# Local attention: the scores of all eight heads in one run with the four masks behind them, minima and exponentials of a step ahead of the copies

## The chip, the core and the metric

The program runs on one core of one Trainium2 chip. The core's engines each execute their own list of instructions strictly in the order written: TensorE (PE in the rows; its weight loads are PEld), VectorE (DVE), ScalarE (ACT), GpSimd (POOL) and SyncE (SP), which issues transfers. The engines are tied to each other by semaphores alone. The metric is the device time of one execution in microseconds.

## What is computed

The reference is a decoder of twelve sublayers on x of 2 x 1024 tokens and 256 features. The change touches the attention inside one of them, L2_ffn, which has two layers of local attention followed by a gated network. Cut to that attention (HEADS = 8, DIM_HEAD = 64, WINDOW = 128, two layers, two sequences):

```python
q = l2norm(q) * qs; k = l2norm(k) * ksc
q, k = rotary_xpos(q, k)
bq = q.reshape(b, h, w, WINDOW, d) * QK_SCALE
...                      # bk, bv: the block before and the block itself
sim = jnp.einsum('bhwid,bhwjd->bhwij', bq, bk)
mask = (i < j) | (i > j + WINDOW) | (j == -1)
sim = jnp.where(mask, -jnp.finfo(sim.dtype).max, sim)
attn = jax.nn.softmax(sim, axis=-1)
out = jnp.einsum('bhwij,bhwjd->bhwid', attn, bv)
```

A block of 128 queries sees the 128 keys of its own block and the 128 before it; the first block sees its own alone.

## The kernel before

The twelve sublayers run one after the other, each made of phases. Within a phase every engine has its own list, and a phase ends with all of them. `local_attention` is such a phase, called four times: for two layers and in each for two sequences, always behind `local_qkv`, which makes QT, KT (queries and keys, features on the partitions, scaled so that the scores have their sign turned) and V.

It goes over NTB = 8 blocks t of 128 queries. The eight heads are four pairs g, and the pairs are two halves G (pairs 0 and 1, pairs 2 and 3). In a step the work on one block is:

- `score(t, G)` on TensorE (line 3542): for two pairs and two heads of each, q times k of 256 keys (128 in step 0) into the four banks 0 to 3, two for each half. Two heads of a pair lie on different rows of the array. Behind them two masks (line 3546, in step 0 line 3549), a bf16 identity times the window mask over the whole bank. It waits for the exponentials of the step before (`exp_done`), since they read the same banks.
- `minima(t, G)` on VectorE (line 3598): the row minimum from a bank with its mask, two a half.
- `exps(t, G)` on ScalarE (line 3655): four a half, from the bank into `probs`, with the row sums beside them. The read of the accumulated sum is an instruction of its own in the rows.
- `recip(t, G)` on VectorE (line 3605), one for a half, and the product with it on GpSimd (line 3641), one for each pair.
- `turn(t, g)` on TensorE (line 3560): four transposes of one pair's probabilities into bank 4 (pairs 0 and 2) or bank 5 (pairs 1 and 3). It waits for the product (`normed`), and until the pair that used the bank before has been copied out (`pt_out_even`, `pt_out_odd`).
- `take_turned(n)`, n = 4 t + g: that copy, of pairs 0 and 2 on VectorE (line 3612), of pairs 1 and 3 on ScalarE (line 3663).
- `values(t)` on TensorE (line 3572): probabilities times V into bank 6 or 7, one step later. `take_out(t)` on VectorE (line 3616) copies the bank to OT.

The order of each list is written out by hand. TensorE's at step t: score(t+1, 0), turn(t, 0), turn(t, 1), score(t+1, 1), values(t-1), turn(t, 2), turn(t, 3). VectorE's: minima(t, 0), the copy of pair 0 of step t-1, minima(t, 1), recip(t, 0), the copy of pair 2 of step t-1, recip(t, 1), take_out(t-2). ScalarE's: exps(t+1, 0), the copy of pair 1 of step t, exps(t+1, 1), the copy of pair 3 of step t.

Of the kernel before, what the change touches and what calls it, by code (L numbers as in the profile page):

```python
# [23 lines left out]
P = 128  # L24
# [3329 lines left out]
LH, LHD = 8, 64  # L3354
# [160 lines left out]
def local_attention(nc, K, b, QT, KT, V, window_mask, OT):  # L3515


    NTB = S // P
    HALVES = LM // 2
    with ExitStack() as es, phase(nc, K.sems, "scored min_done exp_done recip_done normed turned pt_out_even pt_out_odd pv_done out") as (block, s):  # L3520
# [4 lines left out]
        pairs_of = lambda G: (2 * G, 2 * G + 1)  # L3525
# [3 lines left out]
        def turned_probs(n):  # L3529
            t, g = divmod(n, LM)  # L3530
            return (v.rearrange("p (h k) -> p h k", h=2)[:, :, keys(t)] for v in (K.bank[4 + n % 2][:], PT[:, t % 2, g, :]))

        @block.tensor
        def _(pe):
            def score(t, G):
                ks = keys(t)
                if t:
                    pe.wait_ge(s["exp_done"], LH * (t - 1) + 4 * (G + 1))
                for g in pairs_of(G):
                    for hh in range(2):  # L3540
                        own = slice(hh * LHD, (hh + 1) * LHD)
                        pe.matmul(K.bank[2 * G + hh][:, (g % 2) * 2 * P + ks.start:(g % 2 + 1) * 2 * P], QT[own, g, t * P:(t + 1) * P],
                                  KT[own, g, t * P - P + ks.start:(t + 1) * P], start=(g % 2 == 0), stop=False, skip_group_check=True)
                for hh in range(2):
                    if t:
                        ins = pe.matmul(K.bank[2 * G + hh][:], K.identb[:], window_mask[:], start=False, stop=True, skip_group_check=True)  # L3546
                    else:
                        for half in range(2):
                            ins = pe.matmul(K.bank[2 * G + hh][:, half * 2 * P + P:(half + 1) * 2 * P], K.identb[:], window_mask[:, ks],
                                            start=False, stop=True, skip_group_check=True)  # L3550
                    ins.then_inc(s["scored"], 1)

            def turn(t, g):
                n = LM * t + g
                pe.wait_ge(s["normed"], n + 1)
                if n >= 2:
                    pe.wait_ge(pt_out[n % 2], n // 2)
                for hh in range(2):
                    for kt in ((0, 1) if t else (1,)):
                        ins = pe.transpose(K.bank[4 + n % 2][:, (2 * hh + kt) * P:(2 * hh + kt + 1) * P], Pr[:, t % 2, 2 * g + hh, kt * P:(kt + 1) * P], K.ident[:])  # L3560
                ins.then_inc(s["turned"], 1)

            def values(t):
                kts = (0, 1) if t else (1,)
                for g in range(LM):
                    pe.wait_ge(pt_out[g % 2], (LM * t + g) // 2 + 1)
                    if g == 0 and t >= 2:
                        pe.wait_ge(s["out"], t - 1)
                    for hh in range(2):
                        for kt in kts:  # L3570
                            h = 2 * g + hh
                            ins = pe.matmul(K.bank[6 + t % 2][hh * LHD:(hh + 1) * LHD, g * P:(g + 1) * P], V[:, t - 1 + kt, h * LHD:(h + 1) * LHD],
                                            PT[:, t % 2, g, (2 * hh + kt) * P:(2 * hh + kt + 1) * P], start=(kt == kts[0]), stop=(kt == 1))
                    ins.then_inc(s["pv_done"], 1)

            for G in range(HALVES):
                score(0, G)
            for t in range(NTB):
                if t + 1 < NTB:
                    score(t + 1, 0)  # L3580
                for g in pairs_of(0):
                    turn(t, g)
                if t + 1 < NTB:
                    score(t + 1, 1)
                if t:
                    values(t - 1)
                for g in pairs_of(1):
                    turn(t, g)
            values(NTB - 1)

        @block.vector
        def _(dve):
            def minima(t, G):
                if G == 0 and t >= 2:
                    dve.wait_ge(s["exp_done"], LH * (t - 1))
                for hh in range(2):
                    dve.wait_ge(s["scored"], 2 * (HALVES * t + G) + hh + 1)
                    dve.tensor_reduce(stat[:, t % 2, 0, 4 * G:4 * G + 4].rearrange("p (g hh) -> p hh g", hh=2)[:, hh, :],  # L3598
                                      K.bank[2 * G + hh][:].rearrange("p (h k) -> p h k", h=2)[:, :, keys(t)], AX, ALU.min).then_inc(s["min_done"], 1)

            def recip(t, G):
                dve.wait_ge(s["exp_done"], LH * t + 4 * (G + 1))
                if G == 0 and t >= 2:
                    dve.wait_ge(s["normed"], LM * (t - 1))
                dve.reciprocal(stat[:, t % 2, 2, 4 * G:4 * G + 4], stat[:, t % 2, 1, 4 * G:4 * G + 4]).then_inc(s["recip_done"], 1)  # L3605

            def take_turned(n):
                dve.wait_ge(s["turned"], n + 1)
                if n >= 2 * LM:
                    dve.wait_ge(s["pv_done"], n - 2 * LM + 1)  # L3610
                src, dst = turned_probs(n)
                dve.tensor_copy(dst, src).then_inc(s["pt_out_even"], 1)

            def take_out(t):
                dve.wait_ge(s["pv_done"], LM * (t + 1))
                dve.tensor_copy(OT[:, :, b * S + t * P:b * S + (t + 1) * P], K.bank[6 + t % 2][:].rearrange("p (g k) -> p g k", g=LM)).then_inc(s["out"], 1)

            for t in range(NTB):
                minima(t, 0)
                if t:  # L3620
                    take_turned(LM * (t - 1))
                minima(t, 1)
                recip(t, 0)
                if t:
                    take_turned(LM * (t - 1) + 2)
                recip(t, 1)
                if t >= 2:
                    take_out(t - 2)
            for n in (LM * (NTB - 1), LM * (NTB - 1) + 2):
                take_turned(n)  # L3630
            take_out(NTB - 2)
            take_out(NTB - 1)
# [10 lines left out]
        @block.scalar  # L3643
        def _(act):
            def exps(t, G):
                ks = keys(t)
                if t >= 2:
                    act.wait_ge(s["turned"], LM * (t - 2) + 2 * (G + 1))
                    act.wait_ge(s["recip_done"], HALVES * (t - 2) + G + 1)
                for hh in range(2):  # L3650
                    act.wait_ge(s["min_done"], 2 * (HALVES * t + G) + hh + 1)
                    for g in pairs_of(G):
                        h = 2 * g + hh
                        c0 = (g % 2) * 2 * P
                        act.activation(Pr[:, t % 2, h, ks], K.bank[2 * G + hh][:, c0 + ks.start:c0 + ks.stop], ACT.Exp, bias=stat[:, t % 2, 0, h:h + 1],  # L3655
                                       scale=-1.0, accum_out=stat[:, t % 2, 1, h:h + 1]).then_inc(s["exp_done"], 1)

            def take_turned(n):
                act.wait_ge(s["turned"], n + 1)
                if n >= 2 * LM:  # L3660
                    act.wait_ge(s["pv_done"], n - 2 * LM + 1)
                src, dst = turned_probs(n)
                act.activation(dst, src, ACT.Copy).then_inc(s["pt_out_odd"], 1)

            for G in range(HALVES):
                exps(0, G)
            for t in range(NTB):
                for G in range(HALVES):
                    if t + 1 < NTB:
                        exps(t + 1, G)  # L3670
                    take_turned(LM * t + 2 * G + 1)


# [224 lines left out]
```

## Time and profile before

| | us |
|---|---|
| median of 3 runs | 3375.57 |
| lowest and highest | 3375.1, 3379.15 |
| the profiled execution, whole time | 3380.29 |
| its span, first to last instruction | 3378.5 |
| mean granted TensorE clock, as a share of full speed | 0.913 |
| TensorE busy | 2841.4 (84%) |
| VectorE busy | 1865.6 (55%) |
| ScalarE busy | 1601.3 (47%) |
| GpSimd busy | 676.7 (20%) |

The shares are means over twelve sublayers with different limits. What a change inside one phase is worth has to be read from the rows of that phase. A busy TensorE means that matmuls are in flight; they overlap, so the distance between the starts of two of them is what one costs, and the duration of one is longer. The clock is a share of 2.4 GHz, and a stretch at 0.5 runs at 1.2 GHz.

### The profile page before, as it was taken

The page shows a single profiled execution, that of the slowest core. Times are in us where ns is not written, and L with a number is a line of the kernel's source. Part 1 is how long each engine was busy: PE and PEld are TensorE (multiplying, and loading weights), DVE is VectorE, ACT ScalarE, POOL GpSimd, SP SyncE. Part 2 cuts the span into 40 slices and gives each one's busy share as a digit, 9 for nine tenths or more (in the row PEclk, how much of TensorE's full clock was granted, in tenths as well). Part 3 has the DMA queues.
Part 4 walks back from the last instruction along what each step waited for, and adds up shares of the span by engine and source line. Part 5 has one row for each costly group of instructions (what it writes and reads, how often), then busy time and mean ns, then how long its engine had stood idle before and what let it go on. Part 6 is the DMA issues. An engine that isn't in the chain of part 4 may idle for free. (4 is left out here: it accounts for less than half of the span.)

```text
span 3378.5 us, 53803 instructions
## 1 busy us (share of the span) xinstructions
PE 2841.4 (84%) x18568; PEld 1727.8 (51%) x18569; DVE 1865.6 (55%) x4547; ACT 1601.3 (47%) x4391; POOL 676.7 (20%) x757
## 2 busy tenths in 40 slices
PE   7788948638999998679979998999988889959992
PEld 4634633414555555346645563355634356639992
DVE  5655763624887885667656642266423648633333
ACT  5335942314777774772235542155421539713331
POOL 3110020112121120012116630066300003201113
PEclk9879979769999999889999999999999989959996
DMA  1010020010000001000010000000000000141112
GB/s 69 2 18 1 2 82 0 7 62 1 2 2 2 2 2 38 25 13 2 17 40 1 1 34 28 6 1 1 1 28 13 6 23 2 37 197 36 36 35 82
DMA packets 35171, 80.64 MB, mean 24 GB/s; under 512 B 8897, under 2 KB 23826, under 8 KB 30834
## 3 DMA queue, kind: packets, MB, share of 16 engines
q1 hardware_dynamic: 30002, 64.68, 5.3%
q0 software_dynamic: 4368, 11.93, 1.2%
q8 instruction: 137, 2.24, 0.3%
q10 hardware_dynamic: 560, 0.93, 0.1%
q14 instruction: 104, 0.85, 0.1%
HBM read 63.18 MB, written 14.02 MB: 23 GB/s over the span
## 5 line engine op out<-in xcount | busy, mean ns | idle before, releaser
L2459 ACT ACTIVATE scores<-scores,min 128x128 f32<-128x128 f32 (+7 forms) x256 | 198.4, 775 | 86.6 <-DVE min L2442 82.8
L2440 DVE TENSOR_SCALAR zero_marks<-psum 128x128 f32<-128x128 f32 (+7 forms) x256 | 192.1, 751 | 67.9 <-PE psum L2372 65.6
L2442 DVE CUSTOM_DVE_ANT_0 scores<-psum,zero_marks 128x128 f32<-128x128 f32 (+7 forms) x256 | 194.0, 758 | 29.9 <-issue 0.9
L2379 PE MATMUL psum<-ident,scores 128*128 128x128 f32 x1152 | 173.1, 277 | 16.8 <-ACT probsT L2476 13.9
L2476 ACT ACTIVATE probsT<-psum 128x128 f32<-128x128 f32 (+7 forms) x256 | 163.0, 637 | 32.9 <-PE psum L2379 32.3
L3783 PE MATMUL psum<-Hn,W 128*128 128x512 f32 x384 | 169.5, 605 | 8.7 <-PEq L415 8.7
L1597 ACT ACTIVATE XT<-psum,b_of_tile 128x128 f32<-128x128 f32 x312 | 89.0, 368 | 178.8 <-PE psum L1517 178.8
L1517 PE MATMUL psum<-x_gatheredT,XT 128*128 128x128 f32 x1248 | 153.3, 283 | 6.1 <-issue 3.2
L1517 PEld LDWEIGHTS psum<-x_gatheredT,XT 128*128 128x128 f32 x1248 | 148.4, 198 | 12.9 <-issue 11.8
L2379 PEld LDWEIGHTS psum<-ident,scores 128*128 128x128 f32 x1152 | 123.4, 141 | 56.3 <-issue 29.9
L2369 PE MATMUL psum<-XT,Q_heads 64*128 64x512 f32 x256 | 143.7, 641 | 0.0
L3641 POOL TENSOR_TENSOR probs<-probs,stat 128x512 f32<-128x512 f32 (+1 forms) x128 | 123.2, 986 | 98.7 <-DVE stat L3605 96.3
L1526 PE MATMUL psum<-W,XT 128*128 x624 | 141.2, 379 | 0.6 <-DVE y L1571 0.6
L3655 ACT ACTIVATE probs<-psum,stat 128x256 f32<-128x256 f32 (+1 forms) x256 | 114.4, 461 | 47.0 <-DVE stat L3598 45.0
L3783 PEld LDWEIGHTS psum<-Hn,W 128*128 128x128 f32 x384 | 74.3, 194 | 103.9 <-issue 103.9
L3509 POOL TENSOR_TENSOR straight<-straight,crossed 128x512 f32<-128x512 f32 x64 | 81.1, 1268 | 225.2 <-DVE crossed L3499 225.2
L1526 PEld LDWEIGHTS psum<-W,XT 128*128 128x128 f32 x624 | 115.5, 190 | 15.1 <-issue 1.0
L3799 DVE SCALAR_TENSOR_TENSOR GT<-psum,b,gelu 128x512 f32<-128x512 f32 x48 | 36.1, 752 | 141.5 <-ACT gelu L3793 141.5
L848 ACT ACTIVATE probs<-probs,stat 128x154 f32<-128x154 f32 x256 | 104.9, 412 | 2.0 <-DVE stat L786 2.0
L3598 DVE TENSOR_REDUCE stat<-psum 128x2 f32<-128x512 f32 (+1 forms) x128 | 78.2, 653 | 49.4 <-PE psum L3546 27.6
L2370 PE MATMUL psum<-XT,Q_heads_turned 64*128 64x128 f32 (+3 forms) x256 | 102.8, 482 | 0.0
L2363 PE MATMUL psum<-XT,Q_heads 128*128 128x128 f32 (+3 forms) x256 | 97.1, 462 | 3.5 <-POOL Q_heads L2341 2.8
(623 smaller groups left out, 6756.4 us busy)
## 6 DMA issues: line engine op xcount, KB each, us to landing
W<-in_L3f_W SPq DMA_DIRECT2D x16, 1024.0 KB, 22.4
L3f_y_rows<-y SPq DMA_DIRECT2D x39, 128.0 KB, 1.7
L0f_rows<-Xtok SPq DMA_DIRECT2D x2, 2048.0 KB, 7.7
W<-in_L0f_W SPq DMA_DIRECT2D x3, 1152.0 KB
early_weights<-in_L2f_Wqkv SPq DMA_DIRECT2D x2, 1536.0 KB
W<-in_L2f_W SPq DMA_DIRECT2D x2, 1536.0 KB
XT<-in_xT SPq DMA_DIRECT2D x1, 2048.0 KB, 9.2
Xtok<-in_xtok SPq DMA_DIRECT2D x1, 2048.0 KB
```

What stands on the lines that cost most here:

```text
L848: last = act.activation(p, src, ACT.Exp, bias=st(n, 0)[:, h:h + 1], scale=-1.0, accum_out=st(n, 1)[:, h:h + 1])
L1517: ins = pe.matmul(K.bank[2 * q + part][:, m * P:(m + 1) * P], W1t[:, k * INTER + (part * HALF + m) * P:k * INTER + (part * HALF + m + 1) * P],
L1526: ins = pe.matmul(K.bank[6][:, 0:D], HT[:, q, c, :], W2[:, bass.ds(at + c * D, D)], start=(c == 0), stop=(c == IC - 1))
L2369: pe.matmul(sc(i)[:, 0:BLK], Qh[own, u % 2, h, :], KT[own, c, b * S:b * S + BLK], start=True, stop=True, skip_group_check=True)
L2379: ins = pe.transpose(turned[:, kt * P:(kt + 1) * P], Sc[:, i % ROT, kt * P:(kt + 1) * P], K.ident[:])
L2440: dve.tensor_scalar(zero[:, i % 2, 0:n], sc(i)[:, 0:n], 0.0, -NEG, ALU.is_equal, ALU.mult)
L2442: dve.tensor_tensor_reduce(Sc[:, i % ROT, 0:n], sc(i)[:, 0:n], zero[:, i % 2, 0:n], 1.0, -NEG, ALU.add, ALU.min, low[:, i % ROT:i % ROT + ...
L2459: act.activation(p, p, ACT.Exp, bias=low[:, i % ROT:i % ROT + 1], scale=-1.0, accum_out=sums[:, u % 2, h:h + 1]).then_inc(s["exp_done"], 1)
L2476: act.activation(PT[:, i % SLOTS, 0:n], turned[:, 0:n], ACT.Copy).then_inc(s["pt_out"], 1)
L3641: pool.tensor_tensor(v, v, inner(stat[:, t % 2, 2, 2 * g:2 * g + 2], ks.stop - ks.start), ALU.mult).then_inc(s["normed"], 1)
L3655: act.activation(Pr[:, t % 2, h, ks], K.bank[2 * G + hh][:, c0 + ks.start:c0 + ks.stop], ACT.Exp, bias=stat[:, t % 2, 0, h:h + 1], scale=- ...
L3783: ins = pe.matmul(K.bank[2 * (n % 4) + part][:], W1[:, k, (part * HC + m) * P:(part * HC + m + 1) * P], Hn[:, k, j * BLK:(j + 1) * BLK], s ...
```

## The change

It changes the order of three lists and removes or adds no arithmetic. On TensorE `score(t, G)` for the two halves becomes `scores(t)`: the sixteen score matmuls of both halves, then the four masks; it stands where score(t+1, 0) stood, and nothing stands any more where score(t+1, 1) was. Each half still waits for its own exponentials of the step before, but the second half's wait is now ahead of turn(t, 0). On VectorE minima(t, 1) comes ahead of the copy of pair 0 of the step before. On ScalarE exps(t+1, 0) and exps(t+1, 1) come together, and the copies of pairs 1 and 3 behind both.

```diff
-            def score(t, G):
+            def scores(t):
                 ks = keys(t)
-                if t:
-                    pe.wait_ge(s["exp_done"], LH * (t - 1) + 4 * (G + 1))
-                for g in pairs_of(G):
...
-                for hh in range(2):
+                for G in range(HALVES):
                     if t:
-                        ins = pe.matmul(K.bank[2 * G + hh][:], K.identb[:], window_mask[:], start=False, stop=True, skip_group_check=True)
+                        pe.wait_ge(s["exp_done"], LH * (t - 1) + 4 * (G + 1))
+                    for g in pairs_of(G):
+                        for hh in range(2):
...
+                for n in range(2 * HALVES):
+                    if t:
+                        ins = pe.matmul(K.bank[n][:], K.identb[:], window_mask[:], start=False, stop=True, skip_group_check=True)
...
                     ins.then_inc(s["scored"], 1)
...
-            for G in range(HALVES):
-                score(0, G)
+            scores(0)
             for t in range(NTB):
                 if t + 1 < NTB:
-                    score(t + 1, 0)
+                    scores(t + 1)
                 for g in pairs_of(0):
                     turn(t, g)
-                if t + 1 < NTB:
-                    score(t + 1, 1)
                 if t:
                     values(t - 1)
...
             for t in range(NTB):
                 minima(t, 0)
+                minima(t, 1)
                 if t:
                     take_turned(LM * (t - 1))
-                minima(t, 1)
                 recip(t, 0)
...
                 for G in range(HALVES):
                     if t + 1 < NTB:
                         exps(t + 1, G)
+                for G in range(HALVES):
                     take_turned(LM * t + 2 * G + 1)
```

## Rows read from the trace of the kernel before

**Rows 1.** The page: each engine's busy time and share of the span.
```profile
PE 2841.4 (84%) x18568; PEld 1727.8 (51%) x18569; DVE 1865.6 (55%) x4547; ACT 1601.3 (47%) x4391; POOL 676.7 (20%) x757
```

**Rows 2.** Stretches (two phases, one step): start:end, length, busy by engine, granted clock.
```profile
1828.50:1887.30 58.80, 56.74 (x524) 41.17 (x524) 35.58 (x72) 39.30 (x145) 30.80 (x32) 0.94 0.01 2
...
2365.80:2423.90 58.10, 56.12 (x524) 41.00 (x524) 35.66 (x72) 39.24 (x145) 30.81 (x32) 0.96 0.01 2
...
1867.05:1874.10 7.05, 7.05 (x70) 5.18 (x69) 4.61 (x9) 4.93 (x18) 4.08 (x5) 1.00 0.01 2
```

**Rows 3.** One step in order of time: start, length, engine, line [idle before, releaser].
```profile
1867.05 0.60 PE L3546 MATMUL psum<-window_mask,identb 128*128 128x512 bf16 x2
...
1867.49 1.04 PE L3560 MATMUL psum<-ident,probs 128*128 128x128 f32 x8
1867.55 1.29 DVE L3598 TENSOR_REDUCE stat<-psum 128x2 f32<-128x512 f32 x2 [0.54 <-PE psum L3546]
1868.36 0.47 ACT L3655 ACTIVATE probs<-psum,stat 128x256 f32<-128x256 f32 x1 [1.67 <-DVE stat L3598]
...
1868.46 1.13 PE L3542 MATMUL psum<-KT,QT 64*128 64x256 f32 x8
...
1869.53 0.60 PE L3546 MATMUL psum<-window_mask,identb 128*128 128x512 bf16 x2
...
1870.06 2.02 PE L3572 MATMUL psum<-probsT,Xtok 128*64 128x128 f32 x32
1870.16 0.61 ACT L3663 ACTIVATE probsT<-psum 128x512 f32<-128x512 f32 x1
...
1872.01 1.09 PE L3560 MATMUL psum<-ident,probs 128*128 128x128 f32 x8
...
1872.70 0.69 DVE L3612 COPY probsT<-psum 128x512 f32<-128x512 f32 x1 [1.38 <-PE psum L3560]
1873.03 1.14 PE L3542 MATMUL psum<-KT,QT 64*128 64x256 f32 x8
...
1874.10 0.61 PE L3546 MATMUL psum<-window_mask,identb 128*128 128x512 bf16 x2
```

**Rows 4.** Waits from 1852.95 to 1881.15: who for whom, us, times, longest.
```profile
PE psum L3560 <- POOL probs L3641: 0.4, 1, 0.4
```

**Rows 5.** Score matmuls in mid-run, two starts of pairs.
```profile
1873.35 0.59 PE L3542 MATMUL psum<-KT,QT 64*128 64x256 f32 x3
...
1873.57 0.60 PE L3542 MATMUL psum<-KT,QT 64*128 64x256 f32 x4
```

**Rows 6.** The one transpose that waited for ScalarE's copy, in step 0.
```profile
1837.35 0.39 ACT L3663 ACTIVATE probsT<-psum 128x256 f32<-128x256 f32 x1
...
1837.88 0.41 PE L3560 MATMUL psum<-ident,probs 128*128 128x128 f32 x2 [0.43 <-ACT probsT L3663]
```

**Rows 7.** The start of a phase, and the stretch with its clock.
```profile
1831.89 0.21 ACT L3655 ACTIVATION_READ_ACCUMULATOR probs<-psum,stat 128x1 f32 x1
...
1832.16 2.08 PE L3542 MATMUL psum<-KT,QT 64*128 64x256 f32 x8
...
1833.59 0.21 ACT L3655 ACTIVATION_READ_ACCUMULATOR probs<-psum,stat 128x1 f32 x1
...
1834.17 1.03 PE L3546 MATMUL psum<-window_mask,identb 128*128 128x512 bf16 x2
...
1828.20:1835.10 6.90, 6.41 (x35) 4.23 (x36) 2.06 (x7) 4.33 (x18) 2.19 (x4) 0.51 0.02 4
```

**Rows 8.** First masks of steps 2 and 3.
```profile
1839.29 0.39 PE L3546 MATMUL psum<-window_mask,identb 128*128 128x512 bf16 x1
...
1845.90 0.39 PE L3546 MATMUL psum<-window_mask,identb 128*128 128x512 bf16 x1
```

**Rows 9.** The values behind the first turns of step 7.
```profile
1881.59 2.02 PE L3572 MATMUL psum<-probsT,Xtok 128*64 128x128 f32 x32
```

**Rows 10.** A stretch of another stage, columns as in rows 2.
```profile
1415.20:1476.70 61.50, 50.61 (x356) 26.80 (x355) 54.96 (x79) 54.59 (x60) 11.06 (x27) 1.00 0.00 1
```

More of the change, by code:

```diff
@@ L3534, in _ @@
         def _(pe):
-            def score(t, G):
+            def scores(t):
                 ks = keys(t)
-                if t:
-                    pe.wait_ge(s["exp_done"], LH * (t - 1) + 4 * (G + 1))
-                for g in pairs_of(G):
-                    for hh in range(2):
[L3541 to L3544, printed above, removed]
-                    if t:
-                        ins = pe.matmul(K.bank[2 * G + hh][:], K.identb[:], window_mask[:], start=False, stop=True, skip_group_check=True)
+                for G in range(HALVES):
+                    if t:
+                        pe.wait_ge(s["exp_done"], LH * (t - 1) + 4 * (G + 1))
+                    for g in pairs_of(G):
+                        for hh in range(2):
+                            own = slice(hh * LHD, (hh + 1) * LHD)
+                            pe.matmul(K.bank[2 * G + hh][:, (g % 2) * 2 * P + ks.start:(g % 2 + 1) * 2 * P], QT[own, g, t * P:(t + 1) * P],
+                                      KT[own, g, t * P - P + ks.start:(t + 1) * P], start=(g % 2 == 0), stop=False, skip_group_check=True)
+                for n in range(2 * HALVES):
+                    if t:
+                        ins = pe.matmul(K.bank[n][:], K.identb[:], window_mask[:], start=False, stop=True, skip_group_check=True)
                     else:
                         for half in range(2):
-                            ins = pe.matmul(K.bank[2 * G + hh][:, half * 2 * P + P:(half + 1) * 2 * P], K.identb[:], window_mask[:, ks],
+                            ins = pe.matmul(K.bank[n][:, half * 2 * P + P:(half + 1) * 2 * P], K.identb[:], window_mask[:, ks],
                                             start=False, stop=True, skip_group_check=True)
```

## The prediction

> **What bounds the kernel now.** I read the page first, for the share of the local attention in the span, then the table by stretches for its four phases, then one repeating step in order of time, and last the waits. TensorE is busy 84% of the span [rows 1]. The changed code runs in four phases; the longest takes 58.8 us and the shortest 58.1 [rows 2], together some 234 us of the span of 3378.5, so 1% of the whole is 34 us, or 15% of these phases. Within a phase the steps t = 3 to 7 repeat exactly: the first mask of a step follows that of the step before by 7.05 us [rows 3], and the stretch 1867.05 to 1874.10 is one such step, with TensorE busy 7.05 us of 7.05 at a granted clock of 1.00 [rows 2]. The same stretch has DVE at 4.61, ACT at 4.93 and POOL at 4.08. In the waits of a stretch of 28.2 us, three such steps and what follows the last mask, TensorE's matmuls are held 0.4 us in all, by POOL, while the other engines wait for it [rows 4]. So these steps are bound by TensorE's own work, and the room on the other engines is slack, not reserve: ACT is idle 1.67 us in each step before its first exponential [rows 3].
>
> **What a step costs TensorE, and what the new order saves.** Counted from the first mask (time 0 = 1867.05) the rows give: two masks to the first transpose 0.44; eight transposes to the scores 0.97; scores to masks 1.07; masks to values 0.53; values to transposes 1.95; transposes to scores 1.02; scores to masks 1.07; in sum 7.05 [rows 3]. Score matmuls in mid-run start in pairs 0.216 us apart (1873.35 to 1873.57) [rows 5], so four pairs are 0.86, and the other 0.21 of the 1.07 is spent at the two changes of kind. A change from transposes to scores costs a further 0.09 (0.97 less eight transposes at 0.11). One run of all scores with four masks behind it takes one of the two runs of each kind away: 0.21 + 0.09 = 0.3 us saved, a content of **6.75 us** a step. As no other term of work is removed, that is the whole possible gain: 28 steps by 0.3 is 8 us. Bounds: nothing (if the changes cost the same in another place) to 0.4.
> The Trainium skill (TensorE: Matmul & The Clock Gate, "Back-to-back issue gap") prices matmuls by their columns plus a small constant and lists nothing for a change of kind; for the 512-column masks it says some 216 ns, and the rows agree (two in 0.44). By that rule alone the saving is zero; the rows, with 1.07 for 0.86 of scores, speak for 0.2 to 0.3.
>
> **The copies that now come late.** A pair's transposes go to one of two banks, so turn(t, 3) waits until ACT has copied pair 1 of the same step (pt_out_odd), and turn(t, 2) until DVE has copied pair 0. In the new order ACT issues all eight exponentials of step t+1 before that copy, and DVE all four minima before its own. The waits themselves are not new; what is queued ahead of the copy is.
> - *Before*, ACT: copy of pair 1 starts at 1870.16, which is 3.11 after the first mask, behind four exponentials [rows 3].
> - *After*, ACT: mask to first minimum 0.50 (1867.05 to 1867.55); minimum to first exponential 0.81 (to 1868.36); eight exponentials at the pitch of the four that run from 1868.36 to 1870.16, 2 x 1.80 = 3.60; so the copy starts at 4.91. It takes 0.61 [rows 3]. From the end of such a copy to the transpose that waits for it 0.14 (1837.35 + 0.39 to 1837.88) [rows 6]. The transpose may start at **5.66**.
> - *TensorE* would reach it at: four masks 0.88, two turns and change 0.97, values 1.95, one turn 0.49, so 4.29. It is held 1.37 us. Behind it in TensorE's order stand the whole of the next scores, on which the next minima and exponentials wait: the hold is not absorbed but closes a circle.
> - *DVE*: four minima at a pitch of 0.61 (two take 1.29 with the end of the second) from 0.50 end their issue at 2.93; copy 0.69 and release 0.1 give 3.72, against 3.80 at which TensorE reaches turn(t, 2). It just fits; if it is late it is late inside the 1.37 that are lost anyway, so it costs nothing. The reciprocal of the first half follows at 3.6. Now it comes behind the second half's minima, which start behind the mask at 2.48 (1869.53), so not before 4.1; POOL gets its work earlier and stays out of the way.
> - *The scores' own waits*: the second half now asks for all exponentials of step t right at the front. They end at about 5.0, before the held transpose starts. Nothing extra in the steady steps, but in the first ones, below.
> - *values(t-1)* waits for ACT's copy of pair 3, which ACT does while TensorE runs the next scores, as now. Nothing.
>
> **The circle, summed.** First mask to first mask: 0.50 + 0.81 + 3.60 + 0.61 + 0.14, then half of the two turns 0.50, then the run of scores 1.07 + 0.86 = 1.93. Sum **8.09 us**, or from TensorE's side 6.75 + 1.37 = 8.12. Against 7.05 that is **+1.04** a step. The terms with a doubt: the release (0.06, as the scores of step 1 had it behind ACT's last read of its accumulator at 1831.89 + 0.21, to 0.14) [rows 6, 7], the first minimum (0.45 to 0.50), the pitch in a run of eight (0.44 to 0.46); together 7.9 to 8.2.
>
> **A phase, step by step.**
> - *Start to first mask of step 1*: the scores of step 1 now include the second half, which waits for the last exponential of step 0 (its accumulator is read at 1833.59 + 0.21) and runs at a clock of 0.51 [rows 7]. Four pairs at twice 0.216 from 1833.9 reach a mask at about 1835.4, where it was at 1834.17: **+1.2** (0.9 to 1.5).
> - *Step 1 to 2*: before 5.12 (1834.17 to 1839.29) [rows 7, 8]. After: the circle, with a half-size copy (0.39 for 0.61) and half the transposes (0.25 for 0.50), 7.6: **+2.5**.
> - *Step 2 to 3*: before 6.61 [rows 8], after 8.09: **+1.5**.
> - *Four more steps*: 4 x 1.04 = **+4.2**.
> - *Tail*: before, values(6) start 7.49 after the last first mask (1881.59 less 1874.10) [rows 3, 9]. After, turn(6, 3) at 5.66, turn(7, 0) at 6.1, turn(7, 1) behind ACT's copy of pair 3 (6.3 + 0.60 + 0.14) at 7.0, values(6) at 7.5. **0** (from -0.3 to +0.3).
> Together 9.4 us a phase (8.3 to 10.3), and four phases: **+37.6 us** (33 to 41). In step 2 of a phase and before it TensorE was not full, so no cover stands there against the longer circle.
>
> The profiled execution took 3380.29 us with a span of 3378.5, 4.7 above the median of 3375.57. With the sum it would be 3417.9; on the median's footing 3375.6 + 37.6 = **3413 us**.
>
> **Rivals.**
> 1. *TensorE loses its clock in the holes* (slower still). The hole of 1.37 in 8.1 leaves TensorE 83% busy. Each phase starts with a stretch at 0.51 that is 6.9 us long [rows 7]; another such stretch would cost about half its length, 3.4 us, one more in each phase 14 us: 3427, two 3441. Against it: a stretch of 61.5 us elsewhere runs at 1.00 throughout with TensorE busy 50.61 us of it, 82% [rows 10]. The Trainium skill (the same page, "Why this matters for your kernels") warns of idle gaps between bursts of matmuls, after which the clock falls back; by the rows, gaps of this share haven't done so. Chance 0.05.
> 2. *The copy isn't late, TensorE stays the bound* (no change). It decides at 4.29: eight exponentials would have to pass in 2.2 us instead of 3.6. Then the steady steps take 6.75, but the start still pays: +1.2, then +1.0 for step 1 to 2 (0.50 + 0.81 + 3.60 + 0.14 + 1.07 = 6.1 against 5.12), then 4 x -0.3 and some tenths in the tail, 0.3 to 1.0 a phase: 3378. For it speaks that ACT has slack in the sum (4.93 of 7.05); against it, that its slack lies ahead of the first exponential, where it can't be used. Chance 0.04.
> 3. *TensorE-bound from the first step on* (faster). The same, with the scores' wait for all eight exponentials hidden as well: 28 x -0.3 = -8.4, 3367. It needs the chain of 0.50 + 0.81 + exponentials + 1.07 under 5 us. Nothing in the rows has exponentials that fast (a 128x256 one starts every 0.45) [rows 3]. Chance 0.03.
> 4. *The order does part of what it should*: the release is at the short end, the pitch of the exponentials falls in the long run, the early steps hide some; +22 to +27, 3398 to 3402. Chance 0.05.
>
> **How the numbers follow.** The forecast's own case has 0.83 and gives 3404 to 3420 by the bounds of the sum with the 4 us that three runs lie apart; the range reaches on to 3401 and 3425 for terms that I may have missed on either side, and leaves out rivals 1 to 3 and part of 4. A measurement of this kernel can tell about 0.2% (7 us) from no change. Faster by more than that: rival 3, 0.03. Within: rival 2, 0.04. Slower: the rest, 0.93.
>
> **What the profile after would show.** Right: first masks 8.0 to 8.2 us apart in steps 3 to 7; a wait of TensorE for ACT's copy (L3560 for probsT) of 1.2 to 1.4 us in each, some 6 of 7 steps a phase, where now there is 0.4 us once [rows 6]; eight exponentials in one run of 3.6 us followed at once by the copy; phases of 67 to 69 us; TensorE's masks four in 0.88. Wrong on the circle: phases near 58.5 us and no such wait. Wrong on its size: the intervals near 7.5, by a shorter pitch of exponentials. Rival 1: a second stretch at half clock within a phase. Nothing outside the four phases should move, as no DMA and no tile of another stage is touched.

## The result, and the profile after

| | before | after |
|---|---|---|
| median, us | 3377.36 (4 runs) | 3434.80 (4 runs) |
| lowest to highest | 3375.10 to 3381.42 | 3431.64 to 3437.91 |
| the profiled execution | 3380.29 | 3431.64 |
| its span | 3378.5 | 3429.8 |

The ratio is 1.0167 with a 95% interval of 1.0152 to 1.0181: the change costs 57 us. Forecast were 37.6 more, and 3425 as the upper end of the range; the direction and the mechanism of the steady step came as forecast, the size did not.

The stretches of the kernel after: the four attention phases, then one steady step, two stretches at the start of the first phase that follow each other, and the rest of that phase (columns as in rows 2).

```profile
1824.50:1895.05 70.55, 55.91 (x524) 42.15 (x524) 35.28 (x72) 38.82 (x145) 30.63 (x32) 0.95 0.01 2
1950.00:2023.90 73.90, 60.31 (x524) 45.10 (x524) 35.34 (x72) 38.83 (x145) 30.62 (x32) 0.88 0.00 1
2276.00:2348.60 72.60, 58.72 (x524) 43.97 (x524) 35.20 (x72) 38.83 (x145) 30.63 (x32) 0.89 0.00 1
2403.50:2474.60 71.10, 57.18 (x524) 43.30 (x524) 35.19 (x72) 38.86 (x145) 30.63 (x32) 0.92 0.01 1
1873.44:1881.62 8.18, 6.93 (x70) 5.32 (x68) 4.53 (x9) 4.85 (x18) 4.04 (x4) 1.00 0.00 0
...
1828.00:1837.90 9.90, 5.24 (x36) 3.32 (x38) 4.21 (x12) 6.72 (x32) 5.45 (x8) 1.00 0.00 0
1837.90:1841.30 3.40, 3.40 (x15) 1.77 (x12) 0.46 (x1) 0.00 (x0) 0.96 (x1) 0.51 0.00 0
1841.40:1895.05 53.65, 44.14 (x454) 34.43 (x452) 29.46 (x58) 30.27 (x110) 24.22 (x24) 1.00 0.01 2
```

Three things are to be seen against [rows 2]. The phases take 288.1 us where they took 233.9: 54.2 more, against 51.3 in the two spans. So all of the loss lies in them; outside the four phases the two traces differ by 3 us the other way, in code that is the same. The steady step is 8.18 us for 7.05, and TensorE has a hole in it. And the granted clock of the phases is 0.88 to 0.95, where it was 0.94 to 0.96: the first phase has a second stretch at half clock, in the middle of its second step, behind 9.9 us in which TensorE was busy 5.24. In the other three the stretch at half clock that a phase starts with is longer than before (until 10.7, 9.0 and 7.7 us behind the first matmul, for 5.9, 5.8 and 5.2), and each has one or two more behind it.

The steady step after, in order of time (without the accumulator reads):

```profile
1873.44 1.04 PE L3547 MATMUL psum<-window_mask,identb 128*128 128x512 bf16 x4
1873.94 2.48 DVE L3596 TENSOR_REDUCE stat<-psum 128x2 f32<-128x512 f32 x4 [2.83 <-PE psum L3547]
...
1874.32 1.04 PE L3561 MATMUL psum<-ident,probs 128*128 128x128 f32 x8
1874.74 0.47 ACT L3653 ACTIVATE probs<-psum,stat 128x256 f32<-128x256 f32 x1 [2.53 <-DVE stat L3596]
...
1875.28 2.02 PE L3573 MATMUL psum<-probsT,Xtok 128*64 128x128 f32 x32
...
1876.34 0.68 DVE L3610 COPY probsT<-psum 128x512 f32<-128x512 f32 x1
...
1877.23 0.66 PE L3561 MATMUL psum<-ident,probs 128*128 128x128 f32 x4
...
1877.91 0.51 ACT L3653 ACTIVATE probs<-psum,stat 128x256 f32<-128x256 f32 x1
...
1878.36 0.64 ACT L3661 ACTIVATE probsT<-psum 128x512 f32<-128x512 f32 x1
...
1879.13 0.63 PE L3561 MATMUL psum<-ident,probs 128*128 128x128 f32 x4 [1.25 <-ACT probsT L3661]
...
1879.69 2.00 PE L3543 MATMUL psum<-KT,QT 64*128 64x256 f32 x16
1879.80 0.60 ACT L3661 ACTIVATE probsT<-psum 128x512 f32<-128x512 f32 x1 [0.81 <-PE psum L3561]
...
1881.62 0.82 PE L3547 MATMUL psum<-window_mask,identb 128*128 128x512 bf16 x3
```

It is read from the one wait that is new against [rows 3]: TensorE's four transposes of 1879.13 waited 1.25 us, and the row names ScalarE's copy. That copy starts at 1878.36 right behind the eighth exponential (1877.91), while its input was ready since TensorE's eight transposes ended at 1875.36. Forward from there, the transposes hold the scores, the scores the masks (1881.62), and from a mask the chain goes over the first minimum and the exponentials to the next such copy. The copy of VectorE (1876.34 + 0.68) ends ahead of the transposes that need it (1877.23), as forecast.

### The profile page after: what moved, and what is told of

Same layout as the page of the kernel before. It is cut to its first block and busy times, and to the rows that moved or that the text cites. A ratio compares the mean times of both kernels' runs of the same rounds, so it can differ in the third digit from the quotient of the medians.

```text
span 3429.8 us, 53803 instructions
## 1 busy us (share of the span) xinstructions
PE 2846.0 (83%) x18568; PEld 1734.1 (51%) x18569; DVE 1861.5 (54%) x4547; ACT 1600.7 (47%) x4391; POOL 676.4 (20%) x757
## 5 line engine op out<-in xcount | busy, mean ns | idle before, releaser
L3561 PE MATMUL psum<-ident,probs 128*128 128x128 f32 x480 | 70.5, 279 | 47.0 <-ACT probsT L3661 36.7
```

## The experiments

The question of the steady step was which of the three reordered lists sets it; the question of the size was where the rest of the 57 us lies. Theory 1 is the circle through ScalarE's eight exponentials; its rival is that the merged run of scores, with its wait for all exponentials at the front, does it. Theory 2, for the rest, is TensorE's clock, which falls in the holes of a phase's first steps.

**ScalarE's order undone.** The kernel after, with ScalarE's loop of before:

```diff
                 for G in range(HALVES):
                     if t + 1 < NTB:
                         exps(t + 1, G)
-                for G in range(HALVES):
                     take_turned(LM * t + 2 * G + 1)
```

> The changed kernel with one part undone: ScalarE's list is again exps(t+1, 0), copy of pair 1, exps(t+1, 1), copy of pair 3; TensorE's one run of scores and VectorE's order stay changed. Theory 1 (the circle through ScalarE: eight exponentials ahead of the copy that turn(t, 3) waits for): the circle is cut, TensorE is the bound again with its content of 6.75 us a step, no wait of a transpose for ScalarE's copy over 0.2 us; the early steps still pay for the scores' wait for all exponentials, so phases of 58 to 61 us and 3376 to 3390 us in all. Rival (the new order on TensorE costs it, because the second half's scores wait at the front): steps stay at 8.0 us or more and the time at 3425 or more.

Measured: 3386.01 us, ratio to before 1.002 (1.0011 to 1.003). One steady step, and the waits over three of them:

```profile
1864.84:1871.58 6.74, 6.74 (x70) 5.32 (x68) 4.61 (x9) 4.73 (x18) 4.08 (x5) 1.00 0.01 2
```

```profile
ACT probs L3653 <- DVE stat L3596: 5.9, 3, 2.0
DVE stat L3596 <- PE psum L3547: 2.6, 3, 0.9
...
PEld psum L3543 <- ACT probs L3653: 0.5, 3, 0.2
```

The step is 6.74 us, TensorE busy through all of it, and no transpose waits for a copy. The forecast had 6.75 for TensorE's content. So TensorE's order is not what makes the step long; it makes it 0.31 shorter, and undoing one line on ScalarE gives back 49 of the 57 us. The phases take 59.7 to 60.8 us, and they and the time lie inside what was expected.

**ScalarE's order alone.** The kernel before with the loop that this edit puts in:

```diff
                 for G in range(HALVES):
                     if t + 1 < NTB:
                         exps(t + 1, G)
+                for G in range(HALVES):
                     take_turned(LM * t + 2 * G + 1)
```

> The kernel before with one part of the change alone: ScalarE issues exps(t+1, 0) and exps(t+1, 1) ahead of both copies; TensorE and VectorE as before. Theory 1: the step is the same circle without two changes of kind less, 7.9 to 8.1 us; phases of 65 to 69 us, 3408 to 3425 us. Rival (TensorE's order does it): steps stay at 7.05 and the time at 3375 to 3382.

Measured: 3419.54 us, ratio 1.0123 (1.0107 to 1.014), phases of 67.8 to 68.4 us. The held transposes and the first masks around them:

```profile
1872.13 0.60 PE L3546 MATMUL psum<-window_mask,identb 128*128 128x512 bf16 x2
...
1875.84 0.47 ACT L3655 ACTIVATE probs<-psum,stat 128x256 f32<-128x256 f32 x1 [0.47 <-DVE stat L3598]
...
1877.65 0.61 ACT L3663 ACTIVATE probsT<-psum 128x512 f32<-128x512 f32 x1
1878.40 0.63 PE L3560 MATMUL psum<-ident,probs 128*128 128x128 f32 x4 [0.66 <-ACT probsT L3663]
...
1880.03 0.39 PE L3546 MATMUL psum<-window_mask,identb 128*128 128x512 bf16 x1
```

The same wait is there with TensorE's and VectorE's old lists, and the step is 7.90. One line of ScalarE's list is enough for some 39 of the 57 us, here too with one or two stretches at half clock in each phase, beyond 10 us from its first matmul. The step is shorter than 8.18 since only one half's scores stand between the held transposes and the first mask, four pairs or 0.86 less; of that 0.47 comes back as ScalarE now waits for the second half's minima, and the rest of the difference I did not follow.

**TensorE's order alone.** The kernel before with `scores(t)` in TensorE's list as in the change, and both other lists as before:

```diff
             for t in range(NTB):
                 if t + 1 < NTB:
-                    score(t + 1, 0)
+                    scores(t + 1)
                 for g in pairs_of(0):
                     turn(t, g)
-                if t + 1 < NTB:
-                    score(t + 1, 1)
```

> The kernel before with TensorE's part alone: the scores of both halves in one run with four masks behind; ScalarE's and VectorE's lists as before. Theory 1: steps of 6.7 to 6.8 us from step 3 on, 0.3 less than before, as two changes of kind between matmuls are gone; the start of a phase pays 1 to 2.5 us for the scores' wait; 3376 to 3388 us. Rival (TensorE's order is the cause): steps of 8 us, 3425 or more.

Measured: 3387.75 us, ratio 1.0026 (1.0015 to 1.0036). Its first phase and one like it (the second line is of the run above that has VectorE's new order as well, with ScalarE's order undone):

```profile
1824.00:1883.60 59.60, 54.25 (x524) 41.26 (x524) 35.24 (x72) 38.02 (x145) 30.89 (x32) 0.97 0.01 2
```

```profile
1824.40:1884.10 59.70, 53.44 (x524) 41.25 (x524) 35.52 (x72) 38.10 (x145) 30.93 (x32) 0.97 0.01 2
```

They are 0.8 and 0.9 us longer than the 58.8 of [rows 2], and the other phases of the two runs are 1.2 to 2.4 us longer than their like before, though the steady steps are 0.3 shorter. The first mask of step 1 comes 6.9 us behind the phase's first matmul, in other phases of this run up to 8.2, where it came at 5.6; step 1 to 2 takes 6.3 to 6.5 for 4.9 to 5.1. The run of scores that waits for all exponentials loses more at the start, where TensorE has room (14 to 15 us in the four phases up to step 3), than it gains where TensorE is full (some 7 us). VectorE's part of the change makes no difference that these two runs can tell; it was not run alone, nor with ScalarE's new order. The two single changes cost some 39 and 8 us; the other 10 of the 57 come only with both, the step that is 0.28 longer (8.18 for 7.90) among them.

**A ninth exponential, after and before.** In each step from 1 on ScalarE gets one more exponential into a tile that nobody reads:

```diff
+                        if t and G == 0 and hh == 1 and g % 2 == 0:
+                            act.activation(spare[:, t, :], K.bank[2 * G + hh][:, c0:c0 + 2 * P], ACT.Exp, bias=stat[:, t % 2, 0, h:h + 1], scale=-1.0)
```

> The changed kernel with a ninth exponential in each step from 1 on, ScalarE's time of about 0.4 us more (128x256, no sum, into a tile that nobody reads). Theory 1 (ScalarE's run stands in the circle that sets the step): every steady step is longer by the whole of it, 8.5 to 8.65 us for 8.18, phases 2.5 to 3.5 us longer; 3443 to 3450 us. Rival (ScalarE has slack, 4.9 us busy of 8.2, and another thing sets the step): 8.18 as now.

> The kernel before with the same ninth exponential. Theory 1 has TensorE as the bound there, with 1.67 us of ScalarE's idle time ahead of the first exponential: steady steps stay at 7.05 us, the first steps, where the chain through the exponentials counts, lengthen by up to 0.4 each; phases 0.2 to 1.0 us longer, 3377 to 3384 us. Rival (ScalarE's time counts in either order): steps of 7.45 us, 3388 to 3394 us.

Measured: after 3446.82 us (two executions; ratio to before 1.0211, 1.0192 to 1.0229); before 3378.99 us (1.0007, 0.9997 to 1.0017). In the second phase of the first, the extra exponential takes 0.36 us from its start to the next one's, and a step goes from the first mask at 2010.82 to that at 2019.36:

```profile
2010.82 1.04 PE L3548 MATMUL psum<-window_mask,identb 128*128 128x512 bf16 x4
...
2013.48 0.48 ACT L3657 ACTIVATE spare<-psum,stat 128x256 f32<-128x256 f32 x1
2013.84 0.49 ACT L3654 ACTIVATE probs<-psum,stat 128x256 f32<-128x256 f32 x1
...
2019.36 0.82 PE L3548 MATMUL psum<-window_mask,identb 128*128 128x512 bf16 x3
```

It is 8.54 for 8.18, longer by the whole 0.36. The row of the held transposes (2016.87) names GpSimd's product there, but the product that they need was done at 2010.20, and ScalarE's copy ended at 2016.73. The phases did not all come as expected (2.5 to 3.5 us longer): they are 11.1 longer, 1.3 shorter, 2.5 and 4.0 longer, since the stretches at half clock fell differently; the first is looked at in the last section. In the kernel before the same work leaves the step at 7.05:

```profile
1868.00:1875.05 7.05, 7.05 (x70) 5.17 (x68) 4.61 (x10) 5.20 (x19) 4.08 (x5) 1.00 0.01 2
```

ScalarE is busy 4.85 us of 8.18 after the change and 5.20 of 7.05 here. The share says nothing: the less busy one is the one whose every instruction is paid for. With the two edits of ScalarE's list above, this settles theory 1.

**TensorE's holes filled.** The kernel after, with mask matmuls in its holes whose result nobody reads:

```diff
+            def fill(t, n):
+                if t >= 2:
+                    pe.wait_ge(s["out"], t - 1)
+                for _ in range(n):
+                    pe.matmul(K.bank[6 + t % 2][:], K.identb[:], window_mask[:], start=True, stop=True, skip_group_check=True)
...
             scores(0)
+            fill(0, 3)
...
                 if t:
                     values(t - 1)
-                for g in pairs_of(1):
-                    turn(t, g)
+                else:
+                    fill(t, 5)
+                turn(t, 2)
+                if t + 1 < NTB:
+                    fill(t, 4)
+                turn(t, 3)
```

> The changed kernel with idle TensorE time filled: mask matmuls of 512 columns whose result nobody reads go into the free one of banks 6 and 7, three behind the first scores, five ahead of turn(0, 2), four ahead of turn(t, 3) in each step but the last. They add no work to the result. Theory 2 (part of the loss is TensorE's clock: beyond the stretch at the phase's start, it falls to 1.2 GHz again in the holes of the first steps): no stretch at half clock beyond 7 us from a phase's start, steps still 8.1 to 8.3 us, steps 1 to 3 without the 8.6 to 9.9 us that they take now, phases of 67.5 to 70 us, 3412 to 3424 us. Rival (the early steps are long for another reason, and filling only adds work): 3432 to 3445 us.

Measured: 3421.07 us, ratio to before 1.0125 (1.0109 to 1.0142), 13.7 us less than the kernel after, with 36 rows of matmuls more in each phase. Its first phase, and that phase without its first 6.9 us:

```profile
1824.40:1893.60 69.20, 62.15 (x560) 44.75 (x560) 35.26 (x72) 38.78 (x145) 30.59 (x32) 0.98 0.01 2
...
1831.30:1893.60 62.30, 56.21 (x519) 40.47 (x517) 33.49 (x66) 34.61 (x128) 28.64 (x29) 1.00 0.00 1
```

The phases are 68.8 to 69.2 us for 70.6 to 73.9, and no stretch at half clock is left in any of them beyond 5.8 us from the first matmul. Nothing else was changed, so those 12.1 us in the four phases were the clock's. An estimate agrees: by the granted clocks of the stretches the kernel after spends some 51 us of its phases at half clock and the kernel before some 23, and half of the difference is 14 us. The steady steps stay at 8.17 us: they had no clock to win back.

**Where each part of it lies.** With the filled kernel beside the other two, the 54.2 us go as follows (first masks and ends of the four phases, summed):

| | forecast | after, measured | filled |
|---|---|---|---|
| first matmul to first mask of step 1 | +4.8 | +9.0 | +5.6 |
| step 1 to 2 | +10.0 | +16.6 | +10.4 |
| step 2 to 3 | +6.0 | +9.0 | +6.9 |
| step 3 to 7 | +16.8 | +19.0 | +18.7 |
| last first mask to the end | 0 | +0.7 | +0.6 |
| sum | +37.6 | +54.2 | +42.1 |

**Old order first, merged from step 3 on.** `scores` takes the halves that it does as an argument; steps 0, 1 and 2 keep two, later ones have one run. The other lists are as before (the edit is shown against the kernel after):

```diff
-                    scores(t + 1)
+                    scores(t + 1, (0,) if t + 1 <= 2 else (0, 1))
                 for g in pairs_of(0):
                     turn(t, g)
+                if t + 1 <= 2:
+                    scores(t + 1, (1,))
```

> The kernel before with one run of scores only from step 3 on: steps 0, 1 and 2 keep their two halves, ScalarE and VectorE keep their lists. If both the gain (0.3 us of TensorE a step in the steps where it is full) and the loss (the wait for all exponentials in the steps where it is not) are as the earlier runs have them: first mask of step 1 at 5.4 to 5.7 us after the phase's first matmul as before, steps of 6.75 us from step 4 on, phases 0.7 to 1.2 us shorter than before; 3372 to 3378 us beside a kernel before at 3377 to 3380 us, ratio 0.9985 to 0.9995. Rival (the loss of TensorE's run alone, 7 us, is something of every step and not of the first ones): slower than before by 3 to 6 us.

Measured: 3376.75 us, ratio 1.0 (0.9991 to 1.0009). The phases are shorter than before by 0.5 to 1.2 us (its first is the line below), 3 us in all, too little for the medians to tell. The steps from 4 on take 6.74 us, but step 2 to 3, where the first merged run has to wait, takes 7.3 to 7.5 for 6.4 to 6.6, and takes most of the gain of the four steady steps back.

```profile
1824.80:1882.80 58.00, 55.65 (x524) 41.85 (x524) 35.51 (x72) 38.42 (x145) 30.85 (x32) 0.94 0.01 2
```

**The clock at the start of a phase.** Each phase begins at half clock ([rows 7]; 0.50 in the other three). In the phase ahead TensorE has holes before its last turns, which wait for GpSimd, and the clock falls at 1828.2, right behind them. In the kernel before:

```profile
1824.28 0.66 PE L3447 MATMUL psum<-ident,straight 128*128 128x128 f32 x4 [0.73 <-POOL straight L3512]
1826.96 0.66 PE L3447 MATMUL psum<-ident,straight 128*128 128x128 f32 x4 [2.02 <-POOL straight L3512]
```

Matmuls of the first projection fill them:

```diff
+            def warm(count):
+                pe.wait_ge(s["v_out"], NTB - 1)
+                for _ in range(count):
+                    pe.matmul(K.bank[5][:], tile_of(0, NTB - 1), W[:, 0, 0:BLK], start=True, stop=True)
...
+                if n >= N - 3:
+                    warm((2, 1, 4)[n - N + 3])
                 turn(n)
+            warm(2)
```

> The same with extra matmuls in the holes at the end of the projections' phase ahead of each attention phase (two, one and four ahead of the last three turns, two behind the last, 512 columns each, read by nobody). If the half clock at a phase's start comes from TensorE's idle time at the end of the phase ahead: the stretch at half clock that now begins at -0.3 to -1.7 us gets shorter or goes, the first mask of step 1 comes at 4.6 to 5.0 us in the phases where it goes; another 0 to 4 us less, 3369 to 3377 us. If the clock falls for another reason: as the kernel without them, or up to 4 us longer.

Measured: 3375.18 us, ratio 0.9995 (0.9986 to 1.0004). The first phase, and the time to the second:

```profile
1826.40:1882.40 56.00, 52.86 (x524) 40.19 (x524) 35.65 (x72) 38.13 (x145) 30.80 (x32) 1.00 0.01 2
1882.40:1939.30 56.90, 56.37 (x178) 27.73 (x178) 35.77 (x97) 24.51 (x57) 36.67 (x32) 1.00 0.00 1
```

The clock is 1.00 through, and the phases take 55.7 to 56.0 us, 2 us less than without the fillers. The first mask of step 1 comes at 4.05 us, earlier than the 4.6 to 5.0 expected. So the half clock at a phase's start came from TensorE's idle time in the phase ahead. The stretch between two phases, 54.5 us in the kernel before, now takes 56.9: I had counted a 512-column matmul as one of 0.43 us, but in f32 it is two rows of that each (four of them run from 1820.41 to 1823.85 in this trace), and the fillers held the turns. Cut to 256 columns, and three, one, four and two of them:

> One run of scores from step 3 on and extra matmuls at the end of the projections' phase as in the run before, but cut to the holes: matmuls of 256 columns, about 0.43 us each, three, one and four ahead of the last three turns and two behind the last. In the run before, the attention phases were 2.2 to 2.8 us shorter than before and the time between two of them 2.4 us longer, since a 512-column matmul of f32 took 0.86 us there and held the last turns. If that is all: attention phases of 55.7 to 56.2 us with no stretch at half clock, the time between the first two as before (54.5 us) within 0.4; 3366 to 3370 us, ratio 0.997 to 0.998. If the gain was taken back by something else: ratio of 0.999 to 1.000 again.

Measured: **3371.88 us, ratio 0.9978 (0.9969 to 0.9987)**, 0.2% faster than the kernel before, clear of the interval, and 63 us faster than the kernel after. The ratio is in the range expected, the time 2 us above it.

```profile
1823.60:1879.60 56.00, 51.90 (x518) 40.13 (x524) 35.65 (x72) 38.16 (x145) 30.84 (x32) 1.00 0.01 2
1879.60:1934.30 54.70, 53.56 (x180) 27.88 (x181) 36.05 (x96) 24.56 (x58) 36.72 (x32) 1.00 0.00 1
```

The stretch between is back at 54.7. And without the merged scores, the kernel before with these fillers alone:

> The kernel before with the same extra matmuls and no other change. The attention's own orders are untouched, so the phases lose only what the half clock cost at their start: first mask of step 1 at about 4.05 us for 5.6, phases of 56.7 to 57.2 us, 3370 to 3374 us, ratio 0.998 to 0.999. If TensorE's clock at the start cost nothing, because ScalarE's table load and exponentials set the pace there: phases of 58.2 to 58.8 us and a ratio of 1.

Measured: 3375.70 us, ratio 0.9988 (0.9979 to 0.9997); phases of 56.8 us, all four alike, for 58.2 to 58.8 (the time is 2 us above its range, the ratio inside it). The clock at the start is worth 1.4 to 2.0 us a phase, the merged scores 0.8 to 1.1 beside it.

## Why the prediction was right in kind and wrong in size

- *What bounds the kernel*: held. TensorE's 7.05 us are its own work; ScalarE's extra 0.36 us left them alone.
- *TensorE's saving of 0.3 us a step*: held, 6.74 us measured for 6.75. The Trainium skill's silence on a price for a change of kind (TensorE: Matmul & The Clock Gate, "Back-to-back issue gap") would have given 7.05; the runs have the rows' side.
- *The circle*: held as a mechanism, term by term. Mask to minimum 0.50 (forecast 0.50), to the exponential 0.80 (0.81), eight exponentials 3.62 (3.60), copy 0.64 (0.61), release 0.13 (0.14), to the scores 0.56 (0.50), to the mask 1.93 (1.93). Where the 0.06 more in the transposes comes from was not looked into. Sum 8.18 for 8.09; the range for it was 7.9 to 8.2.
- *VectorE's copy and the values*: held, neither is waited for in the steady step.
- *The first mask of step 1 and step 1 to 2*: right where the clock falls no further than before. The filled kernel, at half clock until 3.1 to 5.8 us behind the first matmul, has +1.4 and +2.6 a phase for +1.2 and +2.5. They came as +2.2 and +4.2. **This is the step that failed.** I priced the first steps by their work at the clock that they had before: one stretch at half clock until 5.2 to 6.5 us behind the first matmul, which would stay; the 1835.4 for the first mask comes out only with the clock up again at 1835.1, as in [rows 7], and at half clock to the end it would be 1835.6. The clock's loss on top was put at nothing, and it was 12.1 us. The longer chain of these steps makes TensorE emptier there than in any steady step. The start of the second phase shows it, after and before:

```profile
1950.00:1960.70 10.70, 9.28 (x48) 6.42 (x48) 3.64 (x10) 5.30 (x22) 2.37 (x4) 0.50 0.00 0
```

```profile
1941.80:1947.70 5.90, 5.72 (x33) 3.90 (x34) 1.77 (x6) 4.29 (x17) 1.50 (x3) 0.50 0.00 0
```

In the first phase, from 1828.0 to 1837.9 TensorE is busy 5.24 us of 9.9, and the clock falls at 1837.9, at the start of the run of scores of step 2, and stays down through the rest of it; the run takes 3.12 us for 2.00:

```profile
1834.81 0.41 PE L3561 MATMUL psum<-ident,probs 128*128 128x128 f32 x2 [1.91 <-DVE probsT L3610]
1836.75 0.41 PE L3561 MATMUL psum<-ident,probs 128*128 128x128 f32 x2 [1.53 <-ACT probsT L3661]
1837.09 3.12 PE L3543 MATMUL psum<-KT,QT 64*128 64x256 f32 x16
1840.13 1.56 PE L3547 MATMUL psum<-window_mask,identb 128*128 128x512 bf16 x4
```

- *Rival 1*, the clock, got a chance of 0.05 and came to stand beside the forecast instead of in its place. Its price was about right: one more stretch of 6.9 us a phase, 14 us, against 12.1 measured. In the trace it is a longer first stretch, or one or two more of 3.4 to 6.8 us, or both. The chance was wrong, since I weighed it by the 83% of the steady step and found a stretch of 82% at full clock [rows 10]. In the steady steps that argument held, with no fall there in any of the four phases. It was never applied to steps 0 to 2, although their intervals of 7.6 us, with half the transposes and few values to run in them, stood in the same sum. The Trainium skill's warning of idle gaps between bursts of matmuls (the same page, "Why this matters for your kernels") points at such steps, but it is of longer gaps than any in them. The trace shows more than it states: the clock fell behind two waits of 1.91 and 1.53 us with 0.41 us of matmuls between them.
- *Rivals 2, 3 and 4*: refuted. TensorE waits 1.25 us for the copy in each steady step, and the exponentials' pitch did not fall.
- *What remains*: with the clock taken out, 42.1 us in the phases stand against 37.6: the step's 0.09 and what goes with it from step 2 on (2.8 us by the table), 0.6 in the tail, and 1.2 in the first steps. It lies outside the 33 to 41 of the sum by 1 us. Some 1.1 us of it is on the side of the kernel before: the prediction took the first phase's intervals of 5.12 and 6.61 for all four, and the other three have 4.91 to 5.01 and 6.41. Another 0.7 is one steady step in each of the first two phases, 0.3 to 0.4 longer than its neighbours, from a cause that I did not follow.
- *The medians* differ by 57.4 us and the two profiled spans by 51.3, as the profiled execution before lies 2.9 above its median and the one after 3.2 below. An execution's time goes with its mean granted clock: of the 66 of the kernel before that were taken beside the experiments, the nine at 0.914 took 3372.8 to 3375.8 us and the nine at 0.912 took 3379.4 to 3384.9. The four after have 0.911 (the profiled one, the shortest), 0.910, 0.910 and 0.909. So the clock is likely in this part too, but no trace of a longer execution shows where, and it stays open.
- *The range*: 3401 to 3425. The forecast case and rival 1 together give 3427 by the prediction's own numbers; a range that takes in a cause that can come on top has to add it, not to weigh it as another case.

## What to carry to other kernels

In a kernel like this one, an engine's copy that sets a bank free belongs ahead of its work for the next step, however idle that engine is on average. Ask of each reordered list what was moved in front of an instruction that another engine waits for, and whether that other engine's next output feeds the moved work: then the sum around the circle is the step. And when a chain gets longer, look for the place where TensorE is emptiest, not at the steady step, and add a price for the clock there; a few matmuls that nobody reads, sized by rows to fit the hole, gave back 14 us after the change, and 3 us in the kernel before, where they stand at the end of the phase ahead.

## What the runs showed of the hardware that I had not expected

A step can lock to the clock's fall. In the kernel with the ninth exponential the second to fourth phase run their steady steps at 8.54 us and full clock, but in the first phase of the same execution each of the last five steps takes 10.1 to 10.8 us, with one stretch at half clock in each. Three stretches in a row, half, full, half:

```profile
1868.00:1871.40 3.40, 3.40 (x20) 2.59 (x18) 0.00 (x0) 0.60 (x1) 1.60 (x2) 0.56 0.02 5
1871.50:1878.30 6.80, 5.20 (x55) 3.83 (x52) 4.71 (x9) 4.60 (x18) 2.52 (x3) 0.97 0.00 0
1878.30:1881.70 3.40, 3.40 (x19) 2.46 (x17) 0.00 (x0) 0.60 (x1) 1.51 (x2) 0.56 0.00 0
```

The half clock falls on the run of scores, lengthens the step to 10.2 us, and the next fall meets the next run of scores. The phase took 81.6 us where the second took 72.6. The kernel after has the start of the same in its second phase, with falls in step 1 to 2 and in step 2 to 3, and then none in the steady steps with their holes of 1.25 us, there or in the other three phases; with 1.61 us it was one phase in four, in one trace of each. What decides between the two courses was not tried.
